# A chunked delta-net layer on one NeuronCore: the last level of the triangular inverse as a correction of the mixed matrix, and a new order of the steady steps

## What is computed

```python
def fwd(x):                       # cut to what matters
    q, k, v = silu(causal_conv4(x @ W_qkv.T))      # 16 q/k heads, 32 v heads
    z, a, b = x @ W_z.T, x @ W_a.T, x @ W_b.T
    g, beta = -exp(A_log) * softplus(a + dt_bias), sigmoid(b)
    for t in range(64):                            # state S, 128x128 per value head
        S = S * exp(g[t])
        S = S + outer(k[t], beta[t] * (v[t] - k[t] @ S))
        o[t] = q[t] @ S
    o = rmsnorm(o) * norm_w * silu(z)
    return x + o @ W_out.T
```

## Time and profile before

| | us |
|---|---|
| median of 3 runs | 1622.51 |
| the runs | 1621.43 to 1623.59 |
| the profiled execution, its time | 1629.97 |
| its span | 1628.0 |
| PE busy | 1514.2 (93%) |
| PE weight loads busy | 1075.3 (66%) |
| DVE busy | 1102.7 (68%) |
| ACT busy | 607.5 (37%) |
| POOL busy | 597.1 (37%) |

### The profile page before, as it was taken

One profiled execution on the slowest core, in us unless ns is written; L12 is line 12 of the kernel. 1 busy time (PEld: TensorE's weight loads), 2 busy tenths in 40 slices (PEclk: granted clock), 3 DMA queues, 4 the chain that ended last, 5 costly groups with the idle time before them and its releaser, 6 DMA issues. The chain is left out here.

```text
span 1628.0 us, 34641 instructions
## 1 busy us (share of the span) xinstructions
PE 1514.2 (93%) x14528; PEld 1075.3 (66%) x14528; DVE 1102.7 (68%) x1726; ACT 607.5 (37%) x1028; POOL 597.1 (37%) x935
## 2 busy tenths in 40 slices
PE   6799599999987889999999999999999978999999
PEld 3344278877964557777777677777777765555556
DVE  4767576687567677887788877788787834543433
ACT  3333353345343444344444445444444431111110
POOL 1201143254234457555564546645566421000000
PEclk9999899999998899999999999999999998999999
DMA  8533200110000222121211222112121114100000
GB/s 227 159 105 93 65 1 2 27 27 1 1 1 21 56 50 49 35 49 40 57 46 36 48 44 57 45 36 49 43 57 44 24 28 159 56 1 0 13 1 13
DMA packets 142347, 75.81 MB, mean 47 GB/s; under 512 B 111920, under 2 KB 123440, under 8 KB 140400
## 3 DMA queue, kind: packets, MB, share of 16 engines
q1 hardware_dynamic: 142192, 73.60, 17.6%
HBM read 55.73 MB, written 17.83 MB: 45 GB/s over the span
## 5 line engine op out<-in xcount | busy, mean ns | idle before, releaser
L1894 DVE SCALAR_TENSOR_TENSOR W<-PS,wc,W 128x504 f32<-128x504 f32 x375 | 274.8, 733 | 88.2 <-ACT W L1574 79.3
L1574 ACT ACTIVATE W<-PS,wc 128x512 f32<-128x512 f32 x125 | 85.8, 686 | 173.0 <-PE PS L1269 115.0
L2234 PE MATMUL PS<-HT,wgu 128*128 128x512 f32 x320 | 143.5, 593 | 0.0
L1269 PE MATMUL PS<-HT,wv 128*128 128x512 f32 x252 | 125.1, 620 | 3.4 <-DVE W L1894 3.4
L1441 PE MATMUL PS<-wo,ogT 128*128 128x256 f32 x512 | 119.1, 392 | 7.6 <-DVE dl L1958 5.1
L1292 PE MATMUL PS<-wz,HT 128*128 128x256 f32 x512 | 123.4, 389 | 0.6 <-DMA wz<-in_gdn_w 0.6
L1269 PE MATMUL PS<-HT,wkq 128*128 128x512 f32 x248 | 121.1, 613 | 0.8 <-DVE W L1894 0.8
L2368 DVE SCALAR_TENSOR_TENSOR act<-th,PS 128x512 f32<-128x512 f32 x48 | 33.0, 687 | 128.2 <-ACT th L2294 128.2
L1441 PEld LDWEIGHTS PS<-wo,ogT 128*128 128x128 f32 x512 | 98.6, 195 | 23.9 <-DVE dl L1958 5.3
L1794 POOL TENSOR_TENSOR rr<-nm,con 128x8 f32<-128x8 f32 x16 | 26.5, 1658 | 233.0 <-DVE nm L1923 233.0
L1578 ACT ACTIVATE W<-W 128x512 f32<-128x512 f32 x125 | 78.2, 626 | 89.7 <-DVE W L1894 89.7
(11 more groups left out here) (275 smaller groups left out, 3113.0 us busy)
## 6 DMA issues: line engine op xcount, KB each, us to landing
a_rows<-AT SPq DMA_DIRECT2D x16, 512.0 KB, 2.6
wk<-in_l0x_k SPq DMA_DIRECT2D x16, 384.0 KB, 3.8
wgu<-in_moe_gu SPq DMA_DIRECT2D x5, 1024.0 KB, 15.8
queries_scratch<-tts SPq DMA_DIRECT2D x32, 128.0 KB, 2.7
wkq<-in_gdn_w SPq DMA_DIRECT2D x16, 256.0 KB, 2.8
wv<-in_gdn_w SPq DMA_DIRECT2D x16, 256.0 KB, 2.8
wz<-in_gdn_w SPq DMA_DIRECT2D x16, 256.0 KB, 3.3
wo<-in_gdn_w SPq DMA_DIRECT2D x16, 256.0 KB, 2.9
```

The costliest lines, as they stand in the source:

```text
L1269: mm = pe.matmul(PS[:, qbank(h, q), :], w[:, o:o + DK], HT[:, k, f * 512:(f + 1) * 512], start=(k == 0), stop=(k == DC - 1))
L1574: a.activation(acc[:, flows(h, q), :], PS[:, qbank(h, q), :], ACT.Copy, scale=wc[:, h % 2, 4 * c + 3:4 * c + 4]).then_inc(s["tap"], 1)
L1894: v.scalar_tensor_tensor(a0, p0, wc[:, h % 2, 4 * c + 2 - k:4 * c + 3 - k], a0, ALU.mult, ALU.add).then_inc(s["conv"], 1)
L2234: mm = pe.matmul(PS[:, 2 * (i % 2) + w, :], pack[:, k, w, :], HT[:, k, f * N:(f + 1) * N], start=(k == 0), stop=(k == DC - 1))
```

## The change

The change touches phase 3 only.

- **The last level is no longer put into `T`.** Level 5 would change `T` in its lower left 32x32 quarter alone. Instead `mix` multiplies the `T` of level 4 with `P` into banks 4 and 5, and the missing part is added there: PE computes `A` times the left half of `T` (`lower_cross`), ACT copies it with a negative row mask (`keep_lower`), ACT copies the right half of the mixed matrix (`keep_Z`, new buffer `Zs`), and `correct` multiplies the two and accumulates into the same banks. `turn_T`, `keep_TT`, buffer `TT`, `grow(j, 5)` and `update(j, 5)` go.
- **The first level uses all four quarters.** The results of `cross` for `hv = 1` go to the other half of the partitions (`place`), into bank 7 beside bank 6; `grow` brings them back into the second halves of the two banks. `TT16` takes only the blocks of the odd quarters, each value head by itself.
- **The transfers into `T` are split**: four blocks first (`t16`), then eight into `TT16` (`u16`), then the other four into `T` (`todd`), on which `lower_cross` waits. `load_out` goes behind `blocks_in`.
- `mix` waits for both halves of `P` and is one group. `keep_M` waits for `correct`.
- **The steady steps have another order on PE, ACT and DVE**, `gate` of value head 0 goes to the end of DVE's step, banks of the two value heads' outputs are exchanged, and `gj` is double.

The core of the diff:

```diff
+                def place(hv, b):
+                    return 64 * b if hv == 0 else 64 * (1 - b)
+                def cross(j):
+                    pe.wait_ge(s["t16"], j * 64 + 64)
...
+                    for n in range(TILES):
+                        for b in range(2):
+                            for hv in range(2):
+                                r, w = slice(64 * b, 64 * b + S), place(hv, b)
+                                mm = pe.matmul(PS[w:w + S, 6 + hv, n * 2 * SUB:(n + 1) * 2 * SUB], AT[r, j % 2, hv, n, :],
+                                               left(T[r, :, :, :])[:, hv * TILES + n, :, :], start=True, stop=True)
+                def lower_cross(j):
+                    pe.wait_ge(s["tu"], j + 1)
+                    pe.wait_ge(s["todd"], j * 64 + 64)
...
+                                mm = pe.matmul(PS[w:w + S, 6 + hv, n * 2 * SUB:(n + 1) * 2 * SUB], AT[r, j % 2, hv, n, :], T[r, hv, n, 0:2 * SUB],
+                                               start=True, stop=True)
+                def mix(j):
+                    pe.wait_ge(s["pd"], j * 2 + 2)
...
+                                mm = pe.matmul(PS[w:w + S, 4 + hv, n * S:(n + 1) * S], T[r, hv, n, :], PT[r, j % 2, hv, n, :],
+                                               start=(n == 0), stop=(n == TILES - 1))
+                def correct(j):
+                    pe.wait_ge(s["xs"], j * 3 + 3)
+                    pe.wait_ge(s["zs"], j + 1)
...
+                                w, m = place(hv, b), hv * TILES + n
+                                mm = pe.matmul(PS[w:w + 2 * SUB, 4 + hv, n * S + 2 * SUB:(n + 1) * S], Xs[w:w + S, m, :], Zs[w:w + S, hv, n, :],
+                                               start=False, stop=True, skip_group_check=True)
...
+                def keep_lower(j):
+                    a.wait_ge(s["x"], j * 2 + 2)
+                    a.activation(flat2(Xs[:, :, :]).rearrange("p (h n) -> p h n", h=2), PS[:, 6:8, 0:256], ACT.Copy, scale=C("rows")[:, 2:3]).then_inc(s["xs"], 1)
+                def keep_Z(j):
+                    a.wait_ge(s["mt"], j * 2 + 2)
+                    a.activation(matrices(Zs[:, :, :, :]), wide(4).rearrange("p (m s) -> p m s", s=S)[:, :, 2 * SUB:S],
+                                 ACT.Copy).then_inc(s["zs"], 1)
...
                 def keep_M(j, hv):
-                    v.wait_ge(s["mt"], j * 2 + hv + 1)
+                    v.wait_ge(s["ct"], j + 1)
...
-                    if j > 0:
-                        sp.wait_ge(s["wo"], j * 2)
-                        load_out(j)
                     if h < HK:
                         sp.wait_ge(s["zz"], j * 4 + 4)
                         load_z(h)
                         blocks_in(h)
+                    if j > 0:
+                        sp.wait_ge(s["wo"], j * 2)
+                        load_out(j)
```

More of the change, by code:

```diff
@@ L1753, in last @@
                     scale_wo(g)
-                    keep_X(j, 4)
+                    keep_X(j)
                     tanh_z(j, 2)
-                    for hv in range(2):
-                        keep_TT(j, hv)
-                    keep_X(j, 5)
+                    keep_lower(j)
+                    keep_Z(j)
                     tanh_z(j, 3)
@@ L2016, in step @@
+                    conv(h, 7)
+                    make_P(h, 0)
+                    make_P(h, 1)
+                    silu_z(j, 1)
+                    sum_o(j, 0)
                     silu_z(j, 2)
                     silu_z(j, 3)
-                    gates(j, tail)
-                    if tail:
+                    gate(j, 1)
+                    sum_o(j, 1)
+                    level(j)
+                    silu(h, 6)
+                    if g >= 0:
+                        residual(g, 0)
```

419 lines of the change are left out of this document (173 added, 246 removed).

## The result

The changed kernel takes 1561.76 us, median of 4 runs (1555.6 to 1564.53), against 1623.05 (1621.43 to 1625.5, 4 runs) for the kernel before: a ratio of 0.9616 (95%: 0.9581 to 0.965), 3.8% faster. The forecast was 1566. Its four runs span 0.6%; those of the kernel before span 0.3% here and 0.5% in ten later ones (1622.36 to 1630.88). The profiled execution is the one of 1564.53.

What follows compares the result with a forecast made beforehand. The prediction took PE's own list of work to bound the steady steps. Savings of 46.2 (14 steps at 3.3), 7 (first step) and 3.3 (last step) make 56.5, so 1622.5 - 56.5 = 1566 us, range 1552 to 1596.

Steps and rivals of the forecast that it cites:

- PE's list sets the step: Steady steps: PE works end to end, so a matmul taken away is time taken away; 51.33 us becomes 48.0.
- `turn_T` -1.92: Steady step on PE: the transpose group goes, saving 1.92 us a step.
- `correct` 1.0 in place of 1.99: Steady step on PE: `correct` replaces the second `grow` and takes 1.0 us for 1.99; 0.95 taken as saved.
- the row of 14 ns: Second-stage matmuls with 32-column weights: 14 ns from one to the next, used to price `correct`.
- Four quarters, 0.3 for all: `cross`, `grow`, `lower_cross`: 0.08 us saved each, plus about 0.1 for `mix` behind `lower_cross`; 0.3 a step, between 0 and 0.5.
- The gap at `scores`, 0.2 to 0.5: PE waits 0.2 to 0.5 us for ACT's second `keep_out`, replacing a gap of 0.5; 0.1 saved a step.
- None of the other engines opens a gap: Steady step of 48 us: ACT, DVE, POOL and SP keep up, none with a full microsecond to spare.
- POOL's scaling ends at 7, `turn_out` 1 stands at 10.3: Steady step: POOL's scaling of the outputs is done at 7 us, ahead of `turn_out` 1 on PE at 10.3.
- the third rival: POOL's loop of 41.8 us becomes the bound; 1636 if it took 53; chance 0.07 shared with the order of the quarters.
- First step: `cross` waits 4.5: First step: about 4.5 us of wait for `T`, `outs` about 5.6 earlier; net 7 saved, between 2 and 10.
- Last step -3.3: Last step: net 3.3 us saved, between 1 and 6, with `grow` waiting 2.5 against it.
- that of the chain across the engines: Steady steps: a dozen hand-overs costing 0.1 to 0.25 us more each; step 49.2 to 51, 1583 to 1608; chance 0.13.

Runs made afterwards that it cites:

- q_hv: Changed kernel with the loop over value heads outermost in the five small-matmul groups, so two quarters (diagonal or off it) and one PSUM bank at a time; 1588.66 us, one run.
- q_b: Changed kernel with the loop over b outermost in those five groups, so two quarters of one half at a time and two PSUM banks; 1598.48 us, one run.
- b_mix: Kernel before, with only `mix` changed to one group of 64 in which the value heads alternate over four quarters; 1619.36 us, ratio 0.9967.
- a_keep: Changed kernel with ACT's second `keep_out` moved ahead of one `tanh` and one `tap`; 1549.78 us, ratio 0.9529 to the kernel before.
- a_dma: Changed kernel with four of the eight transfers to POOL's substitution issued by ACT instead of SP, from the third head on; 1563.14 us, ratio 0.9601.
- p_in: `a_dma_keep` with POOL's power and two scaling products moved inside the substitution, ahead of rounds 8 and 12; 1587.69 us, ratio 0.9785.
- a_dma_keep: Changed kernel with the edits of `a_keep` and `a_dma` together; 1541.71 us, ratio 0.9466 to the kernel before.

## Why the prediction was right, and where not

The time came out 4 us below the forecast, inside the range. Of the forecast's own signs, the row of `correct` (1.20) and the wait in the first step (4.58) came as named. `cross` and `grow` did not: 1.14, not 1.9 to 2.0. And PE's gaps stand in four places, ahead of both halves of `turn_out`, of projection 4 and of `scores`, which the prediction had named as a sign that it is wrong. By its own steps:

- *PE's list sets the step.* Right for before; for after only in part, 44.5 of 47.3.
- *`turn_T` -1.92.* The group is gone and nothing took its place. Right.
- *`correct` 1.0 in place of 1.99.* 1.13; saved 0.86 for 0.95. Right, by the row of 14 ns. From the first start to the last it is (1.20 - 0.22) / 63 = 16 ns an instruction. The floor of about 25 ns that the Trainium skill gives ("TensorE: Matmul & The Clock Gate", Back-to-back issue gap), weighed in the prediction, would have made it 1.6; the trace does not bear it out, here and in the 1.14 of the four other groups.
- *Four quarters, 0.3 for all.* The term that failed: 7.76 became 4.15, so 3.6, 0.8 of it in `mix`, which the term did not count. The step in it was "`outs` already uses four and stands at 1.98, so the weights' pace is the limit". `outs` moves 128 columns, the others 32 or 64; I took a row of another moving width as proof that a second cause (quarters) does nothing. The rows before held no group with four quarters and a short moving width, so the bound should have reached down to the row of 14 ns, 0.9 a group. `q_hv`, `q_b` and `b_mix` show it, for 2.7 of the 3.6; the cause of the other 0.9 stays open.
- *The gap at `scores`, 0.2 to 0.5.* 0.72 in most of the steps, 1.45 where both `silu` are late. The chain was laid right as far as ACT's queue goes (`a_keep` takes it away), but `silu` was entered at 0.6, where the earlier trace rows has 0.68, and in part of the steps 2 of them cost 3.1 more.
- *None of the other engines opens a gap.* Failed: 33.7 of idle time in twelve steps. I cited a `silu` of 0.68 and POOL's products of 3.75 as if each were a price of its own. The trace of before had the collision as well, in the very step I read: one `silu` at 906.27 of 1.81 us, inside POOL's products that began at 903.78. The longest one beside the median on that line would have told (min/median/max in ns):

```profile
L1905 DVE SCALAR_TENSOR_TENSOR kvT<-W x61: 681/693/2122, 523.9 to 1288.5; 128x512 f32<-128x512 f32 x61
```

  It was even the old gap ahead of `grow`: in the trace of before, the three steps with a `silu` 0 of 0.68 have no gap there and take 50.54, and the nine others, with 0.93 to 2.12, wait 0.31 to 1.30. In `b_mix`, which has the old order, PE waits there for `Xs` 0.5 to 1.45 in the steps where `silu` 0 lasts 1.3 to 2.3, and not at all for `Xs` where it lasts 0.7 to 1.0.
- *POOL's scaling ends at 7, `turn_out` 1 stands at 10.3.* Counted as there, from the projection (814.21 in the step shown), its second half could have begun at 10.5, but the scaling ended at 11.0 (and at 12.1 in the other kind of step). `A` was issued at 30.6 of the step, not at 28.3, with 3.7 us of gaps ahead of it; so the substitution's last copy ended at 3.5 of the next step, not near 0.5, and the collision added 0.4. A cover of 3 us was eaten by gaps that I had at nothing. This is the wait of 22.5 us, the largest of the new ones. It lies on the loop of the third rival, which was laid at 41.8 of the 48 us; in `a_dma`, where POOL is earlier, it is gone from the steady steps.
- *First step: `cross` waits 4.5.* 4.58. Right. Counted from the first `decay_sums`, `outs` came 10.6 earlier for 5.6, through the shorter groups and a clock that was back up sooner (the first `cross` took 3.63 and the four matmuls behind the wait for DVE 3.78; they take 1.93 and 1.98 now). Then step 1 gave 3.9 back, with 2.88 for DVE and 3.90 for POOL's products, and not 1.2 for `T`. Together -7.8 for -10.3.
- *Last step -3.3.* With the step before it -5.6 for -6.6. `grow` waits 1.26 for 2.5; `turn_out` waits 4.52 for POOL, which was not on the list; the waits for `T` and `Ms` are gone as forecast.

So the forecast's 48.0 a step stands against 47.3 from a list 3 us shorter and gaps 2.4 us longer than laid. The sum was right by luck, by two errors of opposite sign: over the twelve steps some 36 us more gain, and some 29 us more idle time. Of the rivals, that of the chain across the engines described the second error best: hand-overs with half a microsecond to spare gave way in places that I had not priced. What it took of the gain is those 29 us.

What stays open: what decides in a run when POOL's substitution ends, 0.8 us ahead of `decay_sums` or between 0.1 ahead and 0.4 behind it, which by the lock makes the step one of 47.8 or of 46.3. In one profile several steps of one kind follow on each other, so each seems to pass its timing on to the next, but nothing here tests that. The parts of the change were not run one by one either, but for `mix` in `b_mix`; the split over its terms is read from the rows.

## What to carry to other kernels

Price a group of short matmuls by a row that is like it in moving width, in weight width and in the number of quarters of the array that take turns; where no row is, the bound goes down to the fastest row there is. For every operation that is laid at its usual duration, read the longest one on its line as well, and look up what another engine was doing at that time. When PE's list gets shorter, write for every hand-over at which moment each side gets there in the new order: here a third of what the list lost went into waits, though no engine was short of time over the step.

## What the runs showed of the hardware

- 64 short fp32 matmuls with weights 64x64 take 1.85 us where two quarters take turns, (1.85 - 0.22) / 63 = 26 ns from one start to the next, and 1.14 (15 ns) where four do; four quarters give 1.14 with 32 and with 64 moving columns alike. Whether the two are those of a diagonal, of one row half or of one column half, and whether in one or in both PSUM banks, makes no difference in `q_hv` and `q_b`; the kernel before took 2.03 to 2.06 for two quarters on the diagonal and 32 moving columns. With 128 moving columns and four quarters they take 1.98.
- With weights of 64x32 and two quarters, 64 of them take 1.20 us in each of the orders tried.
- POOL's product of SBUF operands and DVE's `silu` with two SBUF operands exclude each other: `silu` 0.69 alone, up to 2.38 beside it; and where `silu` is first, POOL's product waits (2.32 for 1.90). DVE's `conv` with one operand in PSUM was not slowed. POOL's power over 128x8 did not slow `silu` (0.69) but was slowed by it (2.08 for 1.64).
- That power over 128x16 takes 2.9 us on POOL and over 128x8 some 1.6 us, nearly as much as a product over 128x1024 (1.9).
- With one wait of about 3 us a step for PE (`p_in`) the granted clock was 0.96 over the steady steps instead of 1.00, and the same matmuls were 4% longer in sum (527.45 to 547.27). With waits of 1.1 to 1.7 and 0.46 in a step (`a_dma_keep`) it stayed at 1.00. Waits of that size don't decide it: with up to 1.73 and 0.73, it fell in four of twelve steps in `q_b` and in none in `q_hv`, and it fell in one of twelve in the kernel before, whose longest wait there is 1.3.
